# Order of the work behind first halves in a selective-state-space layer kernel

## What is computed

```python
h    = layernorm(x) * (1 + ca) + sa               # x: 1024 tokens x 512
gate = h @ W_gate.T                                # 8192 channels
hBC  = silu(conv4(h @ W_x.T) + conv_b)             # causal convolution, 4 taps along the tokens
y    = scan(hBC, dt, A) + hs * D                   # 128 heads of 64, 8 groups, chunks of 128 tokens
g    = y * silu(gate)
g    = g * rsqrt(mean(g*g over each of 8 groups) + eps) * norm_w
x    = x + ga * (g @ W_out.T)
x    = x + gb * (layernorm(x) * (1 + cb) + sb) @ sign(W_ffn).T + gb * bias
```

## Time and profile before

| what | value |
|---|---|
| median of 3 runs | 1789.65 us (1787.3 to 1790.03) |
| the profiled execution | 1789.48 us |
| its span, first to last instruction | 1787.7 us |
| PE busy | 1730.7 us, 97% |
| DVE busy | 1380.6 us, 77% |
| ACT busy | 1076.4 us, 60% |
| POOL busy | 977.0 us, 55% |

### The profile page before, as it was taken

The page is one execution under the profiler, slowest core; times in us unless marked ns, Lnnn a source line. Parts: engine busy times, 40 slices in busy tenths (PEclk is TensorE's granted clock), DMA queues, the critical chain, the costliest instruction groups (busy, mean ns, idle before and its releaser), DMA issues.

```text
span 1787.7 us, 31728 instructions
## 1 busy us (share of the span) xinstructions
PE 1730.7 (97%) x9798; PEld 1353.3 (76%) x9798; DVE 1380.6 (77%) x2269; ACT 1076.4 (60%) x1826; POOL 977.0 (55%) x732
## 2 busy tenths in 40 slices
PE   6899999999999999999999999999999999999998
PEld 4667778777777777777787777777777777877766
DVE  4777788777877788777887778777887778886786
ACT  6566565666656666565556665566575656566554
POOL 1545564655546575355646555465653647565662
PEclk9899999999999999999999999999999999999999
DMA  6412121111212121021211212121221212212211
GB/s 231 115 28 74 57 74 45 49 57 55 75 33 71 51 70 55 27 74 57 68 51 36 65 56 80 29 74 43 64 62 34 68 51 77 74 51 68 68 48 59
DMA packets 80936, 112.97 MB, mean 63 GB/s; under 512 B 28402, under 2 KB 32498, under 8 KB 79988
## 3 DMA queue, kind: packets, MB, share of 16 engines
q1 hardware_dynamic: 62898, 78.24, 15.0%
q10 hardware_dynamic: 17858, 32.52, 5.4%
HBM read 88.42 MB, written 22.29 MB: 62 GB/s over the span
## 4 chain that ended last, share of the span: by engine, by line
issue 46%; POOL 36%; PE 11%; DVE 3%; ACT 3%; POOLq 1%; DMA 1%; SPq 0%; ACTq 0%; DVEq 0%
POOL yt L1858 10%; POOL ssq L1852 7%; POOL prev L1834 6%; POOL wg_lo L1759 4%; POOL wo_lo L1759 3%; PE bank L518 3%; POOL yt L1861 3%; POOL wx_lo L1759 3%; PE bank L520 2%; PE bank L519 2%; PE bank L779 1%; DMA gate<-w_mod_dram 0%; PE bank L909 0%; PE bank L697 0%; POOL acc L1779 0%
## 5 line engine op out<-in xcount | busy, mean ns | idle before, releaser
L1858 POOL TENSOR_TENSOR yt<-yt,ea 128x384 f32<-128x384 f32 (+1 forms) x126 | 186.4, 1479 | 375.1 <-DVE ea L1642 375.1
L1610 DVE TENSOR_TENSOR lm<-lm,cbm 128x512 f32<-128x512 f32 x256 | 190.0, 783 | 146.0 <-ACT lm L1192 145.2
L1405 DVE SCALAR_TENSOR_TENSOR xc<-bank,bpar,xc 128x511 f32<-128x511 f32 (+2 forms) x384 | 285.5, 743 | 6.8
L518 PE MATMUL bank<-h_hi,wg_hi 128*128 128x512 f32 x640 | 262.4, 410 | 18.1 <-ACT gate L1117 8.1
L520 PE MATMUL bank<-h_hi,wg_lo 128*128 128x512 f32 x640 | 251.2, 393 | 0.0
L519 PE MATMUL bank<-h_lo,wg_hi 128*128 128x512 f32 x640 | 250.7, 392 | 0.0
L518 PE MATMUL bank<-h_hi,wx_hi 128*128 128x512 f32 x512 | 211.8, 414 | 4.1 <-DVE bt L1405 2.2
L1834 POOL TENSOR_TENSOR prev<-prev,dec 128x512 f32<-128x512 f32 x96 | 129.8, 1352 | 156.3 <-DVE prev L1551 91.4
L518 PE MATMUL bank<-wo_hi,g_hi 128*128 128x512 f32 x496 | 206.3, 416 | 0.0
L520 PE MATMUL bank<-h_hi,wx_lo 128*128 128x512 f32 x512 | 201.6, 394 | 0.0
L519 PE MATMUL bank<-h_lo,wx_hi 128*128 128x512 f32 x512 | 200.5, 392 | 0.0
(11 more groups left out here) (238 smaller groups left out, 3956.3 us busy)
## 6 DMA issues: line engine op xcount, KB each, us to landing
raw_w<-w_in_dram SPq DMA_DIRECT2D x145, 256.0 KB, 2.7
raw_w<-w_out_dram SPq DMA_DIRECT2D x64, 256.0 KB, 2.6
part_d<-part ACTq DMA_DIRECT2D x64, 256.0 KB, 2.1
part<-part_d ACTq DMA_DIRECT2D x60, 256.0 KB, 2.7
rt<-rows_d SPq DMA_DIRECT2D x256, 6.0 KB
acc<-x_dram SPq DMA_DIRECT2D x8, 256.0 KB, 6.7
acc<-w_mod_dram SPq DMA_DIRECT2D x2, 1024.0 KB, 6.2
lh<-neg_d SPq DMA_DIRECT2D x128, 6.0 KB
```

The lines of the kernel that those rows point to most:

```text
L518: nc.tensor.matmul(out_ap, whi(k), hhi(k), start=(k == 0), stop=False)
L1405: stt(dst[:, at], ps[:, 0:HALF - 3 + k], w(k), dst[:, at], ALU.mult, ALU.add)\
L1610: tt(lm[:, h % 4, :], lm[:, h % 4, :], cbm[:, toks(hf)], ALU.mult).then_inc(v_m, 1)
L1858: tt(y[:, cols], y[:, cols], ea_tile(end, j)[:, cols], ALU.add).then_inc(p_t3, 1)
```

## The change

The change touches only the part over `j` of first halves. Nothing is computed otherwise, and the instructions are the same in kind and number.

1. DVE: for `j` 2 and 3, `lower_g(j - 1)` comes behind the convolution of that step, and no longer ahead of it. `lower_g(0)` stays where it was (`j == 1`), and `lower_g(3)` still comes last. So `lower_g(2)` and `lower_g(3)` now stand next to each other.
2. ACT, `j == 3`: `split_g` is parted in `round_g` and `square_g`. Now come `round_g(2)`, `tap` of tile 3, `square_g(2)`, silu of gate 0, then the rounding of weight tile 3. Before, it was `g_hi`, square, tap, weight tile, gate.
3. POOL: the low part of weight tile 2 moves from step 2 to step 3, behind the last `g` and ahead of `add_squares(2)`.

```diff
@@ ACT
-                def split_g(j):
+                def round_g(j):
                     se.wait_ge(p_g, 4 * u + j + 1)
...
                     act(g_parts(not more)[0][:, j, :], y, ACT.Copy, scale=par(c // 2, j, NORM)).then_inc(a_hi, 1)
-                    if j == NCT - 1 and not (last and c == 3):
-                        silu_x(u + 1, 3)
+
+                def square_g(j):
...
+                def split_g(j):
+                    round_g(j)
+                    if j == NCT - 1 and more:
+                        silu_x(u + 1, 3)
+                    square_g(j)
...
-                    if j >= 1 and more:
+                    if j == 3 and hf == 0:
+                        round_g(2)
+                    elif j >= 1 and more:
                         split_g(j - 1)
...
                         tap(item, item_bank(n), nv, hv, g + 1, pv)
                         n += 1
+                    if j == 3 and hf == 0:
+                        square_g(2)
+                        silu_gate(u + 1, c + 1, 0)
...
-                            if c < 3:
+                            if c == 1:
                                 silu_gate(u + 1, c + 1, 0)
@@ DVE
-                    if j >= 1 and not end:
+                    if j >= 1 and not end and (hf == 1 or j == 1):
                         lower_g(j - 1)
                     for item in items[j]:
                         conv(item, item_bank(n), nv, hv, g + 1, pv)
                         n += 1
+                    if j >= 2 and hf == 0:
+                        lower_g(j - 1)
@@ POOL
                     tt(y, y, gate[:, j, :], ALU.mult).then_inc(p_g, 1)
+                    for f in todo[2:3] if j == 3 and hf == 0 else []:
+                        unit_fill(f, g)
                     if j >= (2 if c < 2 else 1) and not end:
                         add_squares(j - 1)
-                    for f in todo[j:j + 1]:
+                    for f in todo[j:j + 1] if j != 2 or hf == 1 else []:
                         unit_fill(f, g)
```

More of the change, by code:

```diff
@@ L1213, in split_g @@
                     act(g_parts(not more)[0][:, j, :], y, ACT.Copy, scale=par(c // 2, j, NORM)).then_inc(a_hi, 1)
-                    if j == NCT - 1 and not (last and c == 3):
-                        silu_x(u + 1, 3)
+                def square_g(j):
+                    y = yt_tile(not more, j)
                     if c < 2 and j == 0:
```

## The result

The changed kernel takes 1814.24 us in the median of 4 runs (1813.35 to 1815.98), the kernel before 1789.58 us. The ratio is 1.014, with a 95% interval of 1.0128 to 1.0152: 24.7 us slower, where 22.3 were forecast.

The account below looks back on a forecast made before the run. PE is busy 97% of the span, so whatever makes it wait longer is lost in full. Later last low parts cost 8 x 1.38 + 8 x 1.41 = 22.3 us; 1789.5 + 22.3 = 1811.8 us, range 1797 to 1820.

Parts of the forecast that it names:

- the 1.4 named as a sign: In the trace after, PE idle for about 1.4 us ahead of the output product, ended by `g_lo`, 16 times.
- Rules B and C: DVE ends 0.55 us after POOL's end, POOL then 1.15 after DVE's; between two such DVE instructions POOL's waiting one goes first.
- the pair of masks: Two `lm<-lm,cbm` on DVE in unit `c` 2, with two POOL instructions queued, took 2.65 us: evidence for taking turns.
- Steps 1, 2 and 5: Behind `c` 0: POOL's `yt` takes 1.02 us, step 2's convolution wins only 0.11, and tile 3's convolution wins nothing.
- Steps 3 and 4: Behind `c` 0: `yt` of step 3 starts 0.69 us later, behind `lower_g(1)`; gate projection 2 some 0.2 to 0.3 later.
- Steps 6 and 7: POOL's sum of squares goes between `lower_g(2)` and `lower_g(3)`; the latter ends 1.38 us later (`c` 0), 1.41 (`c` 2).
- What lies beside: Weight tile 3's low part (about 1 us later), next weight load, squares' sum and carried state stay covered by PE's delay.
- Faster without collisions: Rival: `g_lo` takes 0.73 us at its new places, output product 0.69 (`c` 0) or 0.57 (`c` 2) earlier; 1779.4, chance 0.05.
- DVE keeps its turn: Rival: `lower_g(3)` follows `lower_g(2)` at once, 0.34 us late behind `c` 0, 0.37 behind `c` 2; 1795.2, chance 0.06.
- PE makes some up in the second halves: Rival: PE's idle 0.62 and 1.25 us per unit in second halves comes back, 15.0 us in all; 1796.8, chance 0.05.
- One collision more: Rival: DVE's next `xw_lo` meets POOL's last sum of squares, another 0.55 us at each boundary; 1820.6, chance 0.08.
- No change: Rival: losses and gains by halves cancel, 1789.5 us; chance 0.03.

Follow-up runs that it names:

- psum_low: The changed kernel, but lower_g(2) and lower_g(3) of first halves read their second operand from PSUM instead of SBUF; 1791.95 us, ratio 1.0017.
- small_square: The changed kernel, but POOL's addition of the square of tile 2 in first halves covers 8 of 512 columns; 1796.16 us, ratio 1.0046.
- act_pool: The changed kernel with the DVE lines put back, so only the ACT and POOL parts are changed; 1785.66 us, ratio 0.9981 to the kernel before.
- only_low1: The changed kernel with lower_g(2) put back ahead of the last convolution, so only lower_g(1) moves on DVE; 1802.69 us, ratio 1.0075.

## Why the prediction was right, point by point

- **What bounds.** Right. The output product follows the last low part by 0.14 us in both kernels, and the delay of that part went into the time nearly in full. PE's idle time just ahead of the product is 1.2 us and not the 1.4 named as a sign, because part of the delay already falls at the gate (0.59 in the rows above).
- **Rules B and C.** Right in place and size: 0.55 to 0.56 behind POOL's end, and POOL's waiting instruction ahead of DVE's second one. `psum_low` shows that two operands in SBUF are the cause, and `small_square` that neither engine goes twice while the other waits; the pair of masks had told it beforehand.
- **Steps 1, 2 and 5** (POOL's `yt` at 1.02, the convolution of step 2 not really earlier, that of step 3 no gain). Right to 0.1 us and less; only convolution 3 was late with its tap.
- **Steps 3 and 4.** The `yt` of step 3 was mis-sized. I let it start 0.08 us ahead of the recorded end of `lower_g(1)`, as instructions do that follow each other. It starts 0.13 behind it (769.06 + 1.29 = 770.35, then 770.48), so 0.21 later than in my sum. It waits for the semaphore that `lower_g(1)` itself sets, and this is the first place where it stands directly behind it. The gap is 0.13 at 15 of the 16 places (0.50 at one). The wait for POOL does not make it: `lower_g(3)` at 775.88 follows a `lower_g(2)` that had waited as long, and starts 0.08 ahead of its end. The gate was 0.45 us late for the same reason, where I had 0.2 to 0.3. ACT's own terms were right: its square took 0.62 us and the gate 0.58, and the records of the two overlap by 0.10.
- **Steps 6 and 7.** POOL's last three instructions moved with that `yt`: `lower_g(3)` 1.51 instead of 1.38 us late behind `c` 0, 1.58 instead of 1.41 behind `c` 2. 8 x (0.13 + 0.17) = 2.4 us, which is the whole gap between 22.3 and 24.7. The terms fit one by one, so the sum did not come out by errors that cancel.
- **What lies beside.** In the changed kernel the weight tile, the sums and the next loads stayed hidden, because PE was late by as much. The cover was thin: in `act_pool` and `only_low1`, where PE comes earlier, POOL's queue behind the last `g` holds PE.
- **Rivals.** Faster without collisions: refuted by the result, since `lower_g(1)` and both of the pair met POOL in all 16 first halves. Where the two collisions of the pair are gone (`psum_low`) the kernel is 3.4 us slower than before and not 10 faster. DVE keeps its turn: refuted by the pair. PE makes some up in the second halves: 0.4 us, where 15 were costed. One collision more: `xw_lo` did meet POOL's last sum of squares and took 1.05 us at 779.53 instead of 0.69, but PE needs it later, and the time shows nothing of it. Its sum, 1820.6, also lay just outside the stated range, which was meant to hold it. No change: refuted by the result.

## What to carry to other kernels

Before an elementwise instruction on DVE with two operands in SBUF is moved, look at what POOL has queued at its new place: it waits for POOL's instruction to end, and of two such in a row the second waits for the next one as well. Set such instructions apart, as the kernel before does with the convolution between them (each long instruction of which reads PSUM), or give the first of them a place where POOL is idle. And when a wait is taken away, follow the engine past it to the next thing that it reads; here `act_pool` won about a quarter of what the first wait promised (3.3 of 12 us). A busy share is no measure of work where two engines wait for each other in this way.

## What was new about the hardware

- An instruction of 128x8 elements on POOL took 0.66 us in the record, since its time runs from when it is ready and DVE held the port until 766.41; it ended 0.07 us after that. So the recorded length of such an instruction, on POOL or on DVE, is its wait and its work together.
- A DVE instruction that waits for a semaphore set by the DVE instruction just ahead of it started 0.13 us behind that one's end at 15 of 16 places, where without such a wait it starts 0.08 ahead of it.
- Two DVE instructions on 128x512 with one operand in PSUM took 1.40 us beside a busy POOL, with both in SBUF 2.98.
